# Twenty compaction steps of a graph-attention kernel, cut into nine slices of 512 columns with one operand staged in PSUM

## What is computed

```
x = x + conv_attention(layernorm(x))                  # windows of 8 x 8, 8 heads
t = tokens(x);  n = layernorm(t)
h = (n @ W_gat)                                       # 4 heads x 4 experts per node
src, dst = edges + self loops                         # 557,056 pairs
e = leaky_relu(a_src[src] + a_dst[dst])
alpha = segment_softmax(e, dst)                       # per destination node
agg = segment_sum(h[src] * alpha, dst) + b_gat        # the sums need all edges of a node
gate = softmax over the top 2 of mean_heads(layernorm(agg))
t = t + sum_e gate[e] * (gelu(n @ W1[e] + b1[e]) @ W2[e] + b2[e])
```

## Time and profile before

| | |
|---|---|
| median of 3 runs | 8559.0 us (8558.81 to 8560.17) |
| the profiled execution | 8554.89 us, of which the span of its instructions is 8553.0 us |
| POOL busy | 4991.7 us (58% of the span) |
| DVE busy | 3776.7 us (44%) |
| PE busy | 2834.9 us (33%) |
| ACT busy | 1791.7 us (21%) |

### The profile page before, as it was taken

How to read it: one execution, slowest core, us unless ns; L and a number is a source line. 1 busy time by engine, 2 the same in 40 slices (tenths; PEclk the granted TensorE clock), 3 DMA queues, 4 the chain that set the end, 5 groups by cost and what they waited for, 6 DMA issues and landing times.

```text
span 8553.0 us, 47233 instructions
## 1 busy us (share of the span) xinstructions
PE 2834.9 (33%) x14234; PEld 1424.8 (17%) x14234; DVE 3776.7 (44%) x3541; ACT 1791.7 (21%) x2621; POOL 4991.7 (58%) x4876
## 2 busy tenths in 40 slices
PE   2556776666221212112111212121221221200578
PEld 2334444434000000000000000000000000000123
DVE  5998888898332223222322223222121121111699
ACT  1335555443111111111111111111111111110000
POOL 0111112121677777777777777777777777776541
PEclk8778888887665656556565656565665665655555
DMA  1000100000221222222221212121111111111455
GB/s 48 24 25 27 32 30 27 30 27 25 57 70 50 65 55 65 54 59 61 53 66 50 70 50 69 50 70 31 39 39 30 39 39 29 38 26 16 134 185 176
DMA packets 284766, 455.17 MB, mean 53 GB/s; under 512 B 121214, under 2 KB 204382, under 8 KB 262366
## 3 DMA queue, kind: packets, MB, share of 16 engines
q1 hardware_dynamic: 134760, 395.02, 12.7%
q0 software_dynamic: 147648, 56.99, 6.8%
q10 hardware_dynamic: 2208, 1.05, 0.0%
HBM read 231.29 MB, written 221.42 MB: 53 GB/s over the span
## 4 chain that ended last, share of the span: by engine, by line
POOL 52%; issue 18%; DVE 3%; PE 2%; DMA 0%; POOLq 0%; ACT 0%; DVEq 0%
POOL gath L1280 51%; PE bank L1522 1%; DVE yo L1495 1%; POOL got L1557 1%; DVE fin L1500 0%; DMA gate_rows<-gate_dram 0%; DMA gate_dram<-turned_gates 0%; DVE s L1456 0%; DVE sc L1431 0%; POOL first L1707 0%; DVE s L1429 0%; DVE sc L1441 0%; DVE sc L1443 0%; DVE sc L1450 0%; DVE sc L1435 0%
## 5 line engine op out<-in xcount | busy, mean ns | idle before, releaser
L1280 POOL DMA_INDIRECT gath<-node_rows,idx x4352 | 4391.0, 1009 | 1326.3 <-issue 1326.3
L1237 PE MATMUL bank<-xm,w_s 128*128 128x512 f32 x1024 | 625.9, 761 | 4243.3 <-ACT scratch_i L1258 4230.4
L1193 DVE TENSOR_TENSOR adst_in<-bank,gath 128x256 f32<-128x256 f32 x68 | 53.4, 786 | 3372.9 <-DMA gath<-node_rows,idx 3372.9
L1237 PEld LDWEIGHTS bank<-xm,w_s 128*128 128x128 f32 x1024 | 227.0, 240 | 4631.0 <-ACT scratch_i L1258 4486.0
L1261 ACT ACTIVATE bank<-diff 128x256 f32<-128x256 f32 x68 | 26.3, 387 | 4229.7 <-DVE diff L1210 4229.7
L1033 POOL TENSOR_TENSOR scratch_i<-xc,dst_f 128x480 f32<-128x480 f32 x64 | 85.3, 1333 | 1302.1 <-ACT dst_f L950 1302.1
L1180 DVE TENSOR_SCALAR scratch_i<-bank,b_s 128x512 f32<-128x512 f32 x256 | 192.0, 750 | 912.4 <-PE bank L1244 521.9
L1244 PE MATMUL bank<-scratch_i,w_s 128*128 128x512 f32 x1024 | 459.6, 602 | 58.3 <-ACT scratch_i L1258 54.7
L1522 PE MATMUL bank<-gate_rows,choose 4*128 4x512 f32 x512 | 447.4, 1065 | 60.3 <-DVE yo L1495 49.9
L1258 ACT ACTIVATE scratch_i<-bank,b_s 128x512 f32<-128x512 f32 x512 | 344.7, 686 | 253.4 <-PE bank L1237 252.7
L1557 POOL DMA_INDIRECT got<-edge_rows,end_i x256 | 246.3, 962 | 207.2 <-DVE gates L1483 129.5
(11 more groups left out here) (214 smaller groups left out, 5625.6 us busy)
## 6 DMA issues: line engine op xcount, KB each, us to landing
gath<-node_rows,idx POOLq DMA_INDIRECT x4352
y_dram<-scratch_i SPq DMA_DIRECT2D x64, 1024.0 KB, 4.0
yo<-y_dram SPq DMA_DIRECT2D x64, 1024.0 KB, 5.2
edge_rows<-rows SPq DMA_DIRECT2D x68, 768.0 KB, 3.3
line<-moved SPq DMA_DIRECT2D x21, 2048.0 KB, 7.2
moved<-line SPq DMA_DIRECT2D x20, 2048.0 KB
scratch_i<-in_x SPq DMA_DIRECT2D x64, 256.0 KB, 2.8
x_dram<-x SPq DMA_DIRECT2D x64, 256.0 KB, 2.2
```

What stands on the lines that cost most here:

```text
L1237: e.matmul(bank[:, k % 2, :], w1_s[:, k // 2, P * (k % 2):P * (k % 2) + P], xm[par][:, :], start=True, stop=True).then_inc(up_full, 1)
L1280: e.indirect_dma_start(gath[par][:, j, :], None, node_rows, bass.IndirectOffsetOnAxis(ap=idx[par][:, j:j + 1].bitcast(U32), axis=0)).then_ ...
```

## The change

The arithmetic of a step stays the same, but it runs in nine slices, eight of 512 columns and one of 256. ACT copies each arrived slice of `moved` to PSUM bank 4 or 5, converting it to fp32 (`stage_shift`); DVE adds it from there, writes the bits of the slice to the same bank (as int32), multiplies bank by `places` into `moved`, and clears the moved entries by one operation, (bits == 0) * places. ACT's nine copies stand behind the eight Gelus of the chunk, one behind each, the ninth behind the eighth copy. The staging buffers are two banks, so copy n waits until DVE is done with slice n - 2. ACT's chunks 0 to 47 are unrolled.

```diff
+        SLICES = [(a, min(a + 512, EC + TC)) for a in range(0, EC + TC, 512)]
+
+        def staging(n, a, b):
+            return bank[:, 4 + n % 2, 0:b - a]
...
                 k = c // 2 - 1
-                if k:
-                    e.wait_ge(moved_loaded, 16 * 2 * k)
-                    own(e.tensor_tensor(places, places, moved[:, :], ALU.add))
-                settle()
-                if k == PLACE_STEPS:
-                    e.sem_inc(places_done, 1)
-                    return
-                own(e.tensor_scalar(moved[:, :], places, k, 1, ALU.logical_shift_right, ALU.bitwise_and))
-                settle()
-                own(e.tensor_tensor(moved[:, :], moved[:, :], places, ALU.mult))
-                settle()
-                e.tensor_tensor(places, places, moved[:, :], ALU.subtract).then_inc(moved_made, 1)
+                for n, (a, b) in enumerate(SLICES):
+                    now = places[:, a:b]
+                    if k:
+
+                        e.wait_ge(shift_staged, len(SLICES) * (k - 1) + n + 1)
+                        add = e.tensor_tensor(now, now, staging(n, a, b), ALU.add)
+                        if k == PLACE_STEPS:
+                            add.then_inc(shift_merged, 1)
+                            continue
+                        own(add)
+                        settle()
+                    bits = staging(n, a, b).bitcast(I32)
+                    own(e.tensor_scalar(bits, now, k, 1, ALU.logical_shift_right, ALU.bitwise_and))
+                    settle()
+                    own(e.tensor_tensor(moved[:, a:b], bits, now, ALU.mult))
+                    settle()
+                    e.scalar_tensor_tensor(now, bits, 0.0, now, ALU.is_equal, ALU.mult).then_inc(shift_merged, 1)
+                e.wait_ge(shift_merged, len(SLICES) * (k + 1))
+                e.sem_inc(places_done if k == PLACE_STEPS else moved_made, 1)
                 return
...
+        def stage_shift(e, c, n):
+
+            k = c // 2 - 1
+            a, b = SLICES[n]
+            if n == 0:
+                e.wait_ge(moved_loaded, 16 * 2 * k)
+
+            e.wait_ge(shift_merged, len(SLICES) * k + n - 1 if n > 1 else len(SLICES) * k)
+            e.activation(staging(n, a, b), moved[:, a:b], ACT.Copy).then_inc(shift_staged, 1)
...
                     e.activation(hid[:, k, :], bank[:, k % 2, :], ACT.Gelu,
                                  bias=b1_s[:, k // 2, k % 2:k % 2 + 1]).then_inc(hidden, 1)
+                    if shifts:
+                        stage_shift(e, c, k)
+                if shifts:
+                    stage_shift(e, c, 2 * NE)
...
-            with e.Fori(0, EPIECE // 2) as i:
+            for c in range(PLACED):
+                chunk_act(e, c, c % 2, c // 2, True, shifts=c % 2 == 0 and 4 <= c <= PLACE_LAST)
+            with e.Fori(PLACED // 2, EPIECE // 2) as i:
```

More of the change, by code:

```diff
@@ L233, in program @@
         place_step = sem("place_step")
+        shift_staged = sem("shift_staged")
+        shift_merged = sem("shift_merged")
         moved_made = sem("moved_made")
@@ L1250, in copy_indices, with chunk_act @@
             e.activation(idx[par][:, :], keys[1][:, bass.ds(c * U, U)].bitcast(I32), ACT.Copy).then_inc(idx_ready, 1)
-        def chunk_act(e, c, par, i, experts, ahead=True):
+        def chunk_act(e, c, par, i, experts, ahead=True, shifts=False):
             if experts:
```

## The result

The changed kernel takes 8294.2 us (median; 8293.4 to 8297.3) against 8558.9 for the kernel before: a ratio of 0.9691, with a 95% interval of 0.9674 to 0.9708. The forecast was 8295, in a range of 8284 to 8335. The profiled execution has a span of 8291.6 us.

The account below looks back on a forecast made before the run. POOL's one-by-one issue of gathers bounds the kernel. Removing 265.0 us of held gathers, with added work priced at 0, takes 8554.9 to 8289.9, carried to the median 8294, plus 1 for small delays: 8295 us, range 8284 to 8335.

Parts of the forecast that it names:

- What bounds the kernel: POOL issuing 4352 gathers one after another, 5.7 of the 8.55 ms; all other engines wait for it.
- What is removed, 265.0 us: Compaction steps: gathers held by DVE's long operations; 252.3 us in 19 steps, 8.79 in the first, 3.87 at the last add.
- What is added on DVE: 36 short operations per compaction step, at most 0.75 us each, 27 us instead of 16.5; priced as holding no gathers.
- the shape with no row: The bits, one SBUF input and output in PSUM: taken to cost 0, at most 135 us.
- The price of short SBUF operations: Compaction slices: a wrong guess is cheap, as a gather meeting a short operation waits at most 0.75 us.
- If all four kinds stopped gathers: Compaction slices: one gather per two operations, per 1.5 us instead of 1.25; 90 us over 20 steps, 8385 us.
- Rival 2: Compaction: only line 1113 held gathers, not the two-input operations; at most 49 us go, 8510 us; chance 0.02.
- Rival 3: ACT-DVE handshake makes POOL wait for `edge_used`, from steps 97 us beyond 27; 8695 us at 16 us per slice; chance 0.02.
- the 71 us of the double buffer: POOL's further slack after DVE's idle time: it works about 80 us on the chunk between before needing `edge_used`.

Follow-up runs that it names:

- the version above: The changed kernel with the preparing operations of chunks 0 and 1 also in slices through PSUM: 8283.3 us, ratio 0.9677.
- the row with two SBUF inputs: The changed kernel plus one operation with two SBUF inputs over all 4352 columns at the end of each of 20 steps: 8361.5 us, ratio 0.9769.

## Why the prediction was right, and where it was not

**What bounds the kernel: right.** The chain stayed POOL's, and the time followed its gathers: busy time of the group down 262.0 us, the profiled span 261.4; up again by what each added operation held back. The run with 14 more clearings is the exception: there POOL waited.

**What is removed, 265.0 us: right.** It was a sum over 61 long gathers, and all of them are gone. The 11 us of chunks 0 and 1 stayed, and left with the version above. That the median met the forecast to 1 us is partly luck: between the two profiled executions the time fell by 261.2 us, some 4 less than the sum, and the one before lay 4.1 us below its median, the one after 0.5.

**What is added on DVE: right, also for the shape with no row.** The bits into PSUM, bounded by 0 and 135 us, cost 0: in the changed kernel they take 0.69 us for 512 columns, against 0.43 when they go to SBUF, and no gather beside them is longer than usual. For an operation with one input the pace was a good sign of whether it holds gathers; no run separates the pace from the place of the output, which changed with it. The Trainium skill's condition for that pace, "VectorE: DVE Perf Modes", section "What auto-detection actually checks", a single source and the destination in SBUF, agrees with the 0.43 and the 0.69. Operations were sized at 0.75 and took 0.69, copies at 0.69 and took 0.60; the step 24.0 us instead of 27, the idle time left 29.2 instead of 26.

**The price of short SBUF operations: wrong.** "If all four kinds stopped gathers", the prediction said, one gather per two operations, 90 us. At 512 columns in SBUF, the nearest that a run comes to that case, the kernel lost 4. The step that failed took the gathers to walk blindly through a row of operations; in the runs both rows are periodic, and it counts how one period fits the other: 63 us at 384 columns, 4 at 512, 95 at 768. It follows that the gain of this change at 512 columns would have come without PSUM, by the accident of 2.52 against 2.50 us; what PSUM buys is that the width no longer matters, at the two widths tried, 512 and 384.

**Rival 2: out,** as the row with two SBUF inputs shows, 3.4 us each. The Trainium skill, "SBUF — State Buffer", section "Who interferes with whom", says that two SBUF inputs contend with a GpSimd instruction that reads SBUF, and infers that descriptor generation needs only the write interface. Both agree with the two points at which a gather was held if it reads its indices near its start and writes its descriptors near its end; no run here shows that it does. For the operation at double pace, the Trainium skill, on the same page, section "A bandwidth-pool intuition that's wrong (but worth ruling out)" has a DMA "blocked until DVE-end + ~115 ns"; the gathers under way ended 0.12 us behind it.

**Rival 3, its point: wrong.** DVE's idle time and the 71 us of the double buffer were added up as if each step could use both. They can be used once: from step to step the serial chain of two chunks must fit into POOL's 160 us, and beside the 63 us of the rest that leaves a step 97 us, an estimate, not 124. At 74 (8 more clearings) POOL did not wait; at 112 it waited 14 us a pair.

## What to carry to other kernels

Where POOL's indirect DMAs set the time, look for long ones among them and at what DVE runs beside: an operation with two SBUF inputs, or one at double pace, holds the gather that meets it until it ends. It is worth spending more DVE time on forms with one of two inputs in PSUM, or with one input and the output in PSUM, as long as DVE has idle time. Before splitting work over two engines, try the plain form on one. When slicing seems to cure such a hold, change the slice's width once before believing it.

## What was not expected of the hardware

A gather gives way at two points, and differently: 0.82 us before its end to either kind of operation, 0.12 us before its end only to the one at double pace. And two periodic rows of which one can hold the other fall into step: at 768 columns the gathers alternate between 1.28 and 1.56 us for whole steps, at 512 they hardly change.
